# Three gather stages that hand over by fours of chunks instead of one by one

## What is computed

```python
# layer 1, twice (h = x @ W6, then h = h6 @ W7)
norm = edge_weight * rsqrt(deg_out[src] * deg_in[dst] + EPS)
xt = x @ W
msg = xt[src] * norm[:, None]
agg = segment_sum(msg, dst, num_segments=n_nodes)
h = relu(agg + b)
# layer 4
scaled = (X @ W + b) * dinv[:, None]
msg = segment_sum(scaled[col], row, num_segments=N)
out = (msg + scaled) * dinv[:, None]
```

## Time and profile before

| what | us |
|---|---|
| median of three runs | 10909.04 |
| the profiled execution | 10840.75 |
| its span, first to last instruction | 10838.9 |
| stage one, first gather to last add (3416.0 to 4605.6) | 1189.6 |
| stage two (4647.0 to 5814.8) | 1167.8 |
| stage four, first gather to last product (9585.0 to 10784.0) | 1199.0 |

### The profile page before, as it was taken

How to read it: one execution, slowest core, us unless ns; L and a number is a source line. 1 busy time by engine, 2 the same in 40 slices (tenths; PEclk the granted TensorE clock), 3 DMA queues, 4 the chain that set the end, 5 groups by cost and what they waited for, 6 DMA issues and landing times. The chain is left out here.

```text
span 10838.9 us, 118488 instructions
## 1 busy us (share of the span) xinstructions
PE 6703.7 (62%) x28359; PEld 3872.9 (36%) x28359; DVE 6000.7 (55%) x19244; ACT 2968.5 (27%) x9474; POOL 5769.1 (53%) x6086
## 2 busy tenths in 40 slices
PE   3544444455885666666667677775566568956665
PEld 2443333443543433433335111124333334323332
DVE  8555544443003666744444899986555579943333
ACT  1000011111774222200001677773222236600000
POOL 2566666665002676656662688862555520046664
PEclk8666666665998878887777899997666669988887
DMA  3111111111555333333332555552666655523333
GB/s 100 44 44 48 40 47 46 48 45 35 169 173 170 93 94 94 87 116 92 92 92 40 164 173 172 171 143 89 187 192 186 190 132 175 170 71 93 92 92 82
DMA packets 790829, 1189.10 MB, mean 110 GB/s; under 512 B 162029, under 2 KB 633523, under 8 KB 777229
## 3 DMA queue, kind: packets, MB, share of 16 engines
q0 software_dynamic: 246400, 552.44, 19.7%
q1 hardware_dynamic: 543757, 629.10, 17.8%
HBM read 923.59 MB, written 257.40 MB: 109 GB/s over the span
## 5 line engine op out<-in xcount | busy, mean ns | idle before, releaser
L1078 POOL DMA_INDIRECT ring<-scaled_table,idx_s x832 | 787.6, 947 | 1171.6 <-DVEq L188 774.3
L952 POOL DMA_INDIRECT big<-x_table,rec_d_sb x808 | 811.7, 1005 | 1084.5 <-DMA x_table<-big 728.4
L1350 PE MATMUL bank<-ring,wts 128*128 128x512 f32 x1664 | 941.1, 651 | 380.2 <-issue 134.7
L1671 POOL DMA_INDIRECT ring<-att_table,rec_d_sb x808 | 776.4, 961 | 722.9 <-DVE acc L1783 284.4
L307 POOL DMA_INDIRECT rec_s<-acc,big x784 | 790.7, 1009 | 680.6 <-DVE big L532 429.4
L1028 PE MATMUL bank<-iota 128*128 128x512 bf16 x2448 | 1084.7, 443 | 0.0
L1272 POOL DMA_INDIRECT ring<-y_table,idx_s x832 | 812.5, 977 | 396.5 <-DVEq L188 172.9
L307 POOL DMA_INDIRECT rec_d<-x_res,big x784 | 796.4, 1016 | 416.8 <-issue 251.5
L1078 POOL DMA_INDIRECT ring<-h_table,rec_d_sb x808 | 765.6, 948 | 456.4 <-issue 191.8
L441 PE MATMUL bank<-big,wts 128*128 128x25 f32 x3136 | 553.4, 323 | 599.5 <-issue 484.9
L1039 PE MATMUL bank<-big,ring 128*128 128x256 f32 x1616 | 611.3, 467 | 497.8 <-issue 276.7
(11 more groups left out here) (318 smaller groups left out, 14390.7 us busy)
## 6 DMA issues: line engine op xcount, KB each, us to landing
weights_dram<-acc SPq DMA_DIRECT2D x104, 1024.0 KB, 4.5
ring<-weights_dram SPq DMA_DIRECT2D x832, 128.0 KB
rows_spill<-ring SPq DMA_DIRECT2D x808, 128.0 KB
big<-rows_spill SPq DMA_DIRECT2D x808, 128.0 KB, 2.2
ring<-key_dram SPq DMA_DIRECT2D x98, 1024.0 KB
big<-dl_dram SPq DMA_DIRECT2D x50, 512.0 KB
ring<-y_table,idx_s POOLq DMA_INDIRECT x832
ring<-scaled_table,idx_s POOLq DMA_INDIRECT x832
```

The costliest lines, as they stand in the source:

```text
L952: g.indirect_dma_start(out=xg[:, c % RG, :], out_offset=None, in_=x_table, in_offset=bass.IndirectOffsetOnAxis(ap=recd3i[:, c, D_IDX:D_IDX ...
L1078: g.indirect_dma_start(out=slot[:, c % ring_len, :], out_offset=None, in_=table, in_offset=bass.IndirectOffsetOnAxis(ap=index(c), axis=0)) ...
L1350: pe.matmul(ps[6 + u % 2], oh1[c // 4 % 2][:, c % 4, :], mid[:, c % 2, 0:512], start=(c % GS == 0), stop=(c % GS == GS - 1)).then_inc(summ ...
L1671: g.indirect_dma_start(out=ag[:, n % R3, :], out_offset=None, in_=att_table, in_offset=bass.IndirectOffsetOnAxis(ap=recd3i[:, n, D_IDX:D_I ...
```

## The change

- **One signal for four.** In all three stages PE increments `summed` only at the last of four chunks, and what waits on it counts fours (group m is the chunks 4m to 4m+3). The one-hots are also told by fours (`weighed` or `hot_made` at the last of four), and PE waits for them once in four chunks. PE still waits for each chunk's gathered rows.
- **Two products in a bank.** The four products of a group lie in two banks, side by side (`half_bank`); three groups take six banks. In stage four a bank holds the two sums of a group, and seven banks are used.
- **Rings.** Stage one: the weighted one-hots become three fours (`fours`, 12 in place of 8); the 24 slots stay. Stages two and four: 16 one-hots in place of 4 (now in the tensor `acc`, behind the accumulator), 20 slots of gathered rows in place of 12.
- **Distances.** Stages two and four add at a distance of 8 chunks, in place of 2 and 3. In stage one ACT's and DVE's distances stay as they are.
- **Order within DVE.** In stages two and four `added` is told once in a group, and the wait of an add for the add before it becomes an explicit `drain`. Stage two begins with a wait for twenty small DMAs that stage one's start has issued.

```diff
@@ stage one: POOL, DVE, ACT
-                if c >= RG:
-                    g.wait_ge(summed.s, summed.n(c - RG + 1))
+                if c >= RG and c % 4 == 0:
+                    g.wait_ge(summed.s, summed.n((c - RG) // 4 + 1))
...
                 c = n - 16
                 if c >= 0:
-                    v.wait_ge(summed.s, summed.n(c + 1))
+                    if c % 4 == 0:
+                        v.wait_ge(summed.s, summed.n(c // 4 + 1))
...
                 c = n - 12
                 if c >= 0:
+                    m = c // 4
                     a.wait_ge(normed.s, normed.n(c // 8 + 1))
-                    if c >= 8:
-                        a.wait_ge(summed.s, summed.n(c - 7))
-                    a.mul(onehot[:, c % 8, :], dst_hot[c // 8 % 3][:, c % 8, :],
-                          norm[:, c:c + 1]).then_inc(weighed.s, 1)
+                    if m >= 3 and c % 4 == 0:
+                        a.wait_ge(summed.s, summed.n(m - 2))
+                    ins = a.mul(fours[m % 3][:, c % 4, :], dst_hot[c // 8 % 3][:, c % 8, :], norm[:, c:c + 1])
+                    if c % 4 == 3:
+                        ins.then_inc(weighed.s, 1)
+
+        def half_bank(c):
+
+            return ps[c // 4 % 3 * 2 + c % 4 // 2][:, c % 2 * D:c % 2 * D + D]
@@ stage one: PE
                 pe.wait_ge(gathered.s(c, RG), gathered.n(c, RG))
-                pe.wait_ge(weighed.s, weighed.n(c + 1))
-                if c >= 7:
-                    pe.wait_ge(added.s, added.n(c - 6))
-                pe.matmul(ps[c % 7][:, 0:D], onehot[:, c % 8, :], xg[:, c % RG, 0:D],
-                          start=True, stop=True).then_inc(summed.s, 1)
+                if c % 4 == 0:
+                    pe.wait_ge(weighed.s, weighed.n(m + 1))
+                    if m >= 3:
+                        pe.wait_ge(added.s, added.n(4 * (m - 2)))
+                ins = pe.matmul(half_bank(c), fours[m % 3][:, c % 4, :], xg[:, c % RG, 0:D], start=True, stop=True)
+                if c % 4 == 3:
+                    ins.then_inc(summed.s, 1)
@@ stage two: DVE (stage four alike)
-        R2 = 12
+        R2 = 20
...
-            for n in range(NCD + 2):
+            v.wait_ge(rows_out[0].s, 16 * 12)
+            v.wait_ge(rows_out[1].s, 16 * 8)
+            for n in range(NCD + 8):
                 if n < NCD:
-                    if n >= 4:
-                        v.wait_ge(summed.s, summed.n(n - 3))
-                    v.tensor_scalar(hot4[:, n % 4, :], ...).then_inc(weighed.s, 1)
-                c = n - 2
+                    if n >= 16 and n % 4 == 0:
+                        v.wait_ge(summed.s, summed.n(n // 4 - 3))
+                    ins = v.tensor_scalar(hot16[:, n % 16, :], ...)
+                    if n % 4 == 3:
+                        ins.then_inc(weighed.s, 1)
+                c = n - 8
                 if c >= 0:
-                    v.wait_ge(summed.s, summed.n(c + 1))
+                    if c % 4 == 0:
+                        v.wait_ge(summed.s, summed.n(c // 4 + 1))
                     if c >= 1:
-                        v.wait_ge(added.s, added.n(c))
+                        v.drain()
                     here = acc[:, bass.ds(blk.at(c) * D, D)]
-                    v.tensor_tensor(here, here, ps[c % 7][:, 0:D], ALU.add).then_inc(added.s, 1)
+                    ins = v.tensor_tensor(here, here, half_bank(c), ALU.add)
+                    if c % 4 == 3:
+                        ins.then_inc(added.s, 1)
```

More of the change, by code:

```diff
@@ L1007, in first_vector @@
                     here = acc[:, bass.ds(blk1.at(c) * D, D)]
-                    v.tensor_tensor(here, here, ps[c % 7][:, 0:D], ALU.add).then_inc(added.s, 1)
+                    v.tensor_tensor(here, here, half_bank(c), ALU.add).then_inc(added.s, 1)
         def first_scalar():
@@ L1048, in program @@
         gathered.over(NCD, RG)
-        weighed.over(NCD)
-        summed.over(NCD)
+        weighed.over(NCD // 4)
+        summed.over(NCD // 4)
         added.over(NCD)
@@ L1099, in second_tensor @@
+                    if c % 4 == 3:
+                        ins.then_inc(added.s, 1)
         def second_tensor():
             for c in range(NCD):
+                m = c // 4
                 pe.wait_ge(gathered.s(c, R2), gathered.n(c, R2))
[L1102 to L1106, removed]
+                if c % 4 == 0:
+                    pe.wait_ge(weighed.s, weighed.n(m + 1))
+                    if m >= 3:
+                        pe.wait_ge(added.s, added.n(m - 2))
@@ L1132, in program @@
         gathered.over(NCD, R2)
-        weighed.over(NCD)
-        summed.over(NCD)
-        added.over(NCD)
+        weighed.over(NCD // 4)
+        summed.over(NCD // 4)
+        added.over(NCD // 4)
         meet()
@@ L1993, in fourth_vector @@
             blk = Numbers(v, regs_v, blk_s_row, NB - 1)
-            for n in range(NCS + 3):
+            for n in range(NCS + 8):
                 if n < NCS:
[L1996 to L2000, removed]
+                    if n >= 16 and n % 4 == 0:
+                        v.wait_ge(summed.s, summed.n(n // 4 - 3))
+                    ins = v.tensor_scalar(oh16[:, n % 16, :], iota, sl_s[:, n:n + 1], None, ALU.is_equal)
+                    if n % 4 == 3:
+                        ins.then_inc(hot_made.s, 1)
+                c = n - 8
@@ L2001, in fourth_vector @@
                 if c >= 0 and c % GS == GS - 1:
-                    u = c // GS
-                    v.wait_ge(summed.s, summed.n(c + 1))
+                    m, u = c // 4, c // GS
+                    if u % 2 == 0:
+                        v.wait_ge(summed.s, summed.n(m + 1))
                     if u >= 1:
-                        v.wait_ge(added.s, added.n(u))
+                        v.drain()
                     here = acc[:, bass.ds(blk.at(u) * D, D)]
-                    v.tensor_tensor(here, here, ps[3 + u % 4][:, 0:D], ALU.add).then_inc(added.s, 1)
+                    ins = v.tensor_tensor(here, here, ps[m % 7][:, u % 2 * D:u % 2 * D + D], ALU.add)
@@ L2009, in fourth_tensor @@
+                    if u % 2 == 1:
+                        ins.then_inc(added.s, 1)
         def fourth_tensor():
             for c in range(NCS):
-                u = c // GS
-                pe.wait_ge(hot_made.s, hot_made.n(c + 1))
+                m, u = c // 4, c // GS
                 pe.wait_ge(gathered.s(c, R4), gathered.n(c, R4))
[L2014 to L2017, removed]
+                if c % 4 == 0:
+                    pe.wait_ge(hot_made.s, hot_made.n(m + 1))
+                    if m >= 7:
+                        pe.wait_ge(added.s, added.n(m - 6))
@@ L2018, in fourth_tensor @@
+                ins = pe.matmul(ps[m % 7][:, u % 2 * D:u % 2 * D + D], oh16[:, c % 16, :], sg[:, c % R4, :],
+                                start=(c % GS == 0), stop=(c % GS == GS - 1))
+                if c % 4 == 3:
+                    ins.then_inc(summed.s, 1)
                 spare_product()
         def end_vector():
-            v.wait_ge(added.s, added.n(NUS))
+            v.wait_ge(added.s, added.n(NUS // 2))
             for b in range(NB):
```

23 lines of the change are left out of this document (13 added, 10 removed).

## The result

The changed kernel takes 11089.03 us (median of four runs, 11075.21 to 11095.88) against 10913.5 us of the kernel before on the same chip. The ratio is 1.0138, with a 95% interval of 1.0098 to 1.0179: slower, by less than the 2% that the text counted as no change. The profiled execution has a span of 11094.1 us.

A forecast was written before the change was run, and what follows sets the result against it. The prediction took waits for PE's late signals, above POOL's own pace, as the bound. Stage one +300 and stages two and four -245 summed to +55 us: median 10909 to 10964, 8-in-10 range 10760 to 11170.

The forecast's parts named there:

- +300: Stage one: eight products on the path where four were, 14.6 us a batch, +3.0 us in each of 101 batches.
- -245: Stages two and four: -125 and -120 us, as gathers come near POOL's own pace; bounds -285 and -195.
- rival D: Whole kernel: lateness goes, but PE at lower clock and episodes leave half the gain, -125; total +175, 11084 us; chance 0.10.
- with L = 1.0: Stage one: the group's signal from PE to DVE comes 1.0 us late, making a batch 14.6 us.
- The chain without it: Stage one's batch without signal lateness: PE's start, eight products, hand-over, half a register load, adds to next batch; 13.6 us.
- there is little queue, and each signal is late by what one alone is late: Stages two and four: one PE signal for four cuts lateness to 1.0 us, bounds 0.16 and 2.8.
- Rival C: Whole kernel: a lone signal is as late as queued ones, perhaps from gathers in flight; +240 and more, 11150 us; chance 0.16.
- POOL becomes the bound, and 20 slots cover it: Stages two and four: POOL's 1.25 us a gather sets the pace, floor 1013 and 1043 us; 20 slots hold 25 us.
- The rule on serialized increments: All stages: semaphore increments serialize at some 26 ns each; three fewer in each of 612 groups, 48 us at most.

The follow-up runs named there:

- one_by_one_stage1: Changed kernel with stage one as before (every weighting and product told singly, ring of 8): 9093.14 us against 9100.3 of the kernel before, ratio 0.9999.
- told_singly_to_pe: Changed kernel, but in stage one ACT tells each weighted one-hot singly and PE waits for each: 12.62 us a batch against 13.63.
- pe_tells_singly: Changed kernel, but in stage one PE tells each product singly, each in its own bank: 12.72 us a batch against 13.63.
- weigh_two_earlier: Changed kernel with ACT's weighting in stage one at distance 10 in place of 12: 11.96 us a batch against 13.63.
- before_no_spare: Kernel before without the spare products in its three stages: 10786.04 us against 10817.21 of the kernel before.
- before_again: Kernel before, unchanged, run again for its profile: 10820.66 us beside 10816.99 of the kernel before.

## Why the prediction was right or wrong

**The time.** 11089 us lies inside the range of 10760 to 11170, but 125 us above the 10964 forecast. The terms were further off than their sum: stage one +199 where I had +300, stages two and four +5 where I had -245. It is near rival D's 11084 by number only. D still had -125 in it, and nothing of that came.

**Stage one: mechanism right, size too large.** The step that was mis-sized is the lateness, "with L = 1.0", 14.6 us a batch. The chain without it, 13.6, is what was measured (13.63), because the group's signal follows in 0.17 us. On chip 4, where one_by_one_stage1 runs stage one as before at 10.65 us a batch, the same change costs 2.98 us a batch. That the group cuts the batch in two places was argued; told_singly_to_pe, pe_tells_singly and weigh_two_earlier show it, at 1.0, 0.9 and (on chip 4) 1.7 us a batch. Eight products partly at the lower clock after 6.2 us of idleness came as said: a product takes 1.19 or 1.06 us at first and 0.59 at the end, and all eight 7.6 us (4210.79 to 4218.39).

**Stages two and four: the step that failed** is "there is little queue, and each signal is late by what one alone is late", taken as 1.0 us between 0.16 and 2.8. The lateness in the timeline above is 9.0 us, outside both bounds. I had read the 2.84 us between two late adds as a queue of signals, and drew the gain from shortening it. The number of PE's signals does not set the pace: four times fewer left it at 1.434 us. Rival C's mechanism, the gathers in flight, is what the runs bear out for these stages: without gathers the lateness is gone on a chip that had it, and with PE's work varied from none to two spare products it stays. C's number, 11150, failed in stage one, where it had signals late which are prompt.

The row that I passed over stood in my own argument: POOL's pace was 1.435 us in stage two and 1.425 in stage four, although the one told a signal for each chunk and added at distance 2, and the other added once in two chunks at distance 3. Two different loops with one pace point to a limit that belongs to neither. Stage one has it too, 1166.8 / 807 = 1.446 us.

"POOL becomes the bound, and 20 slots cover it" was worked out rightly for a prompt signal: on chip 4 the stages take 1010 and 1040 us (I had 1013 and 1043). But there the kernel with one signal a chunk is no slower (one_by_one_stage1 against the kernel before, 0.9999), so the change has nothing to gain on either kind of chip.

**The rule on serialized increments** (the Trainium skill, TensorE: Matmul & The Clock Gate, The cost: per-tile semaphore tail) is stated there for tiles packed into the array. I had weighed it at 48 us at most. In stages two and four nothing of it shows in the time; no run here measures an increment by itself.

**What stays open.** Shown is that PE's signals are late only beside gathers, and that gathers of half the rows or half the bytes leave the pace where it was. By which way a gather delays a signal is not shown, nor whether the price is one of each gather, nor why one chip is free of it and four others are not. The changed kernel as it stands was not run on chip 4, nor stage one told singly on both sides on one of the other chips. No version found beats the kernel before: before_no_spare, 0.998, has an interval that holds 1.

## What to carry to other kernels

When a group of chunks becomes the unit of a hand-over, look for other periodic work with which it shares an engine's order (here a root and a reduction once in eight chunks): each place where the group straddled it here put two more products on the path, and that cost was there on both kinds of chips, while a gain from fewer signals has to be shown first. Before pricing a late signal, find out what it is late from: compare the pace of stages whose loops differ, and run one with the suspected traffic taken out. Here the pace that was the same for unlike loops moved by 1% with the ring's depth and not at all with the count of signals.

## What was unexpected

- Two kinds of chips: the same kernel takes 9100 us on one and 10817 to 10945 on the others. Stages with gathers account for part of it (1010 against 1150 us in stage two); without gathers stage two takes 752 us on both.
- On the slower kind the gathers of stages two and four followed at 1.42 to 1.45 us on average in every form tried: 64 or 128 rows, 512 or 1024 bytes a row, rings of 12 or 20, one signal for one or for four products, one add for one or for two chunks. On the other kind it was 1.250.
- A signal of PE's came 9.0 us after the product's end in the middle of gathers, and 0.17 us after it in stage one of the same execution, where gathers are 1366.3 / 807 = 1.69 us apart. Two runs on chip 1 bear on why. In pe_tells_singly, with gathers 1.58 us apart, single signals are mostly prompt (a median of 0.16 us, 50 of 348 over 1 us), where before_again, with gathers 1.45 us apart, has a median of 5.1 us. So the slower pace of gathers goes with prompt signals even when PE tells singly. With fours at 1.57 us, told_singly_to_pe has 1 of 150, so fewer signals may help a little too. Neither was varied by itself.
